# Second rows kept in pairs, their differences formed on GpSimd: attention and router kernel, 1 core

## The reference, cut to what matters

```python
xn = layernorm(x)                                # x: (4, 512, 512), 16 tiles of 128 rows
qkv = silu(xn @ w_qkv.T); gate = sigmoid(xn @ w_gate.T)      # 16 heads of 128
# per head: causal attention with decay in 64-row blocks, a state kv carried over
o = norm_w * o * rsqrt(mean(o * o) + 1e-6)
s = (gate * o) @ w_out.T
w8, i8 = top_k(softmax(xn @ router_weight.T + router_bias), 8)
g = silu(xn * sum(w8) + w8 @ expert_bias[i8])
return x + s * g
```

## Time and profile before

| | |
|---|---|
| three runs | 1120.8, 1121.27, 1123.83 us; median 1121.27 |
| profiled execution | 1121.57 us, its span 1119.7 us |
| mean granted clock of PE | 0.997 |
| PE busy | 1096.1 us, 98% of the span |
| DVE | 844.3 us, 75% |
| ACT | 608.8 us, 54% |
| POOL | 108.2 us, 10% |
| DMA queue of SP | 84.41 MB, 23.4% of 16 engines |
| chain of waits | PE 82%, DVE 13%, ACT 3%, issue 1% |

### The profile page before, as it was taken

The page is one execution under the profiler, slowest core; times in us unless marked ns, Lnnn a source line. Parts: engine busy times, 40 slices in busy tenths (PEclk is TensorE's granted clock), DMA queues, the critical chain, the costliest instruction groups (busy, mean ns, idle before and its releaser), DMA issues.

```text
span 1119.7 us, 16260 instructions
## 1 busy us (share of the span) xinstructions
PE 1096.1 (98%) x6367; PEld 953.0 (85%) x6367; DVE 844.3 (75%) x1637; ACT 608.8 (54%) x1308; POOL 108.2 (10%) x99
## 2 busy tenths in 40 slices
PE   8899999999999999999999999999999999999997
PEld 6788889898898978889788797888988889898886
DVE  7778787776878778786777888868678787766757
ACT  4566474555646455474445655546555564655542
POOL 4001000000000001101010000000000000000002
PEclk8999999999999999999999999999999999999999
DMA  4313121222211223222122341211212032121404
GB/s 136 104 52 104 47 76 60 62 88 57 94 38 58 94 95 112 97 66 85 48 76 79 118 153 57 85 48 48 76 48 76 29 95 66 38 67 47 141 1 132
DMA packets 37566, 85.46 MB, mean 76 GB/s; under 512 B 4320, under 2 KB 8688, under 8 KB 37488
## 3 DMA queue, kind: packets, MB, share of 16 engines
q1 hardware_dynamic: 37488, 84.41, 23.4%
HBM read 73.88 MB, written 14.71 MB: 79 GB/s over the span
## 4 chain that ended last, share of the span: by engine, by line
PE 82%; DVE 13%; ACT 3%; issue 1%; DMA 0%; POOL 0%; SPq 0%; DVEq 0%
PE psR L216 45%; PE psB L216 19%; PE psO L216 8%; PE psS L216 8%; PE psS L647 1%; DVE wvl L394 1%; DVE yacc L790 1%; DVE xl L304 1%; ACT zh L730 1%; DVE gl L394 1%; DVE T L725 1%; DVE T L672 1%; DVE yacc L819 1%; DVE wt L458 1%; ACT ph L674 1%
## 5 line engine op out<-in xcount | busy, mean ns | idle before, releaser
L747 POOL TENSOR_TENSOR ss<-ss,sq 128x512 f32<-128x512 f32 x58 | 78.5, 1353 | 828.6 <-ACT sq L731 828.6
L216 PE MATMUL psR<-xh,gh 128*128 128x512 f32 x384 | 128.6, 416 | 4.8 <-DVE xs L980 2.6
L730 ACT ACTIVATE zh<-T,nw 128x512 fp32r<-128x512 f32 x64 | 46.3, 724 | 136.7 <-DVE T L725 136.7
L216 PE MATMUL psR<-xl,gh 128*128 128x512 f32 x384 | 119.3, 392 | 0.0
L216 PE MATMUL psR<-xh,gl 128*128 128x512 f32 x384 | 118.7, 390 | 0.0
L216 PE MATMUL psB<-xh,gh 128*128 128x512 f32 x288 | 92.8, 403 | 1.2 <-DVE psR L557 1.2
L394 DVE TENSOR_TENSOR gl<-raw,gh 128x256 fp32r<-128x256 f32 x144 | 86.0, 598 | 7.1 <-ACT gh L393 4.7
L216 PE MATMUL psB<-xl,gh 128*128 128x512 f32 x288 | 89.3, 391 | 0.0
L216 PE MATMUL psR<-wvh,xh 128*128 128x256 f32 x512 | 87.3, 293 | 2.0 <-DVE xl L304 1.9
L216 PE MATMUL psB<-xh,gl 128*128 128x512 f32 x288 | 88.8, 390 | 0.0
L674 ACT ACTIVATE ph<-T 128x512 fp32r<-128x512 f32 x64 | 40.5, 632 | 87.6 <-DVE T L672 87.6
(11 more groups left out here) (199 smaller groups left out, 2691.1 us busy)
## 6 DMA issues: line engine op xcount, KB each, us to landing
raw<-w SPq DMA_DIRECT2D x80, 512.0 KB, 3.5
D<-dtab SPq DMA_DIRECT2D x32, 256.0 KB, 2.6
xs<-x SPq DMA_DIRECT2D x28, 256.0 KB, 2.8
dtab<-dscr SPq DMA_DIRECT2D x16, 256.0 KB
gscr<-xs SPq DMA_DIRECT2D x16, 256.0 KB, 2.0
xs<-xnorm SPq DMA_DIRECT2D x16, 256.0 KB, 3.8
out_dram<-yacc SPq DMA_DIRECT2D x16, 256.0 KB, 2.3
xs<-gscr SPq DMA_DIRECT2D x14, 256.0 KB, 3.9
```

Source lines behind the costliest of these rows:

```text
L216: return lambda e: e.matmul(o, l, r, start=start, stop=stop, skip_group_check=shared)
L730: hi = act.do(lambda a: a.activation(zh[:, i, :], T[:, t, :], ACT.Copy, scale=half), z, nw_ev, *zfree)
L747: a = lane.do(lambda g: g.tensor_add(ss[:, j, :], ss[:, j, :], sq[:, :]), q, ss_ev.get(j))
```

## The change

The four differences of each pair of second rows are no longer formed on DVE when the phase changes. They are formed when the rows are kept, on GpSimd, in place in the two row buffers, and stored to a new DRAM tensor `xmixed` (8 tiles of 128 x 512). At the change of phase both `xnorm` and `xmixed` are loaded, one buffer of the ring after the other (`get(count)`).

The eight keepings move from eight consecutive hooks (from (5, 4) on) to four visits: statistics at (0,0), (0,2), (0,3), (1,0), (6,2), (6,3), (6,4), (7,0), for tiles 8, 12, 9, 13, 10, 14, 11, 15. The load stands two hooks ahead of the statistics, or at (0, 0) for the first two. Normalising and the store to `xnorm` now come one hook behind the statistics, and `keep_mixed` comes two hooks behind the second tile of a pair: at (0, 4), (1, 2), (7, 0), (7, 2).

```diff
+    xmixed = nc.dram_tensor("xmixed", (B * N // 2, H), F32, kind="Internal").ap()
...
-            def keep(tt=tt):
-                i, ld = held.pop(tt)
-                stat(tt, i, ld)
-                e = normalise(tt, i, ld)
-                xn_ev[tt] = sp.dma(xs_port[i], xnorm[tt * P:(tt + 1) * P, :], xs[:, i, :], e)
-                xring.give(i, xn_ev[tt])
-
-            later(*step((5, 2), k), load)
-            later(*step((5, 2), k + 2), keep)
...
+        def keep(tt):
+            i, ld = held.pop(tt)
+            e = normalise(tt, i, ld)
+            xn_ev[tt] = sp.dma(xs_port[i], xnorm[tt * P:(tt + 1) * P, :], xs[:, i, :], e)
+            held[("n", tt)] = i
+
+        def keep_mixed(t):
+
+            i, j = held.pop(("n", 8 + t)), held.pop(("n", 12 + t))
+            xa, xb = row(i), row(j)
+            lo, hi = slice(0, 256), slice(256, 512)
+            e = pool.do(lambda g: g.tensor_sub(xa[:, lo], xb[:, lo], xa[:, lo]), xn_ev[8 + t], xn_ev[12 + t])
+            pool.do(lambda g: g.tensor_sub(xb[:, lo], xb[:, lo], xb[:, hi]), e)
+            e2 = pool.do(lambda g: g.tensor_sub(xb[:, hi], xb[:, hi], xa[:, lo]), e)
+            e4 = pool.do(lambda g: g.tensor_sub(xa[:, hi], xa[:, hi], xb[:, hi]), e2)
+            for n, slot, tt in ((2 * t, i, 8 + t), (2 * t + 1, j, 12 + t)):
+                xc_ev[n] = sp.dma(xs_port[slot], xmixed[n * P:(n + 1) * P, :], xs[:, slot, :], e4)
+                xring.give(slot, xc_ev[n])
+
+        KEPT = ((0, 0), (0, 2), (0, 3), (1, 0), (6, 2), (6, 3), (6, 4), (7, 0))
+        for at, tt in zip(KEPT, (8, 12, 9, 13, 10, 14, 11, 15)):
+            later(*step(at, -2 if at[0] or at[1] > 1 else 0), lambda tt=tt: load(tt))
+            later(*at, lambda tt=tt: stat(tt, *held[tt]))
+            later(*step(at), lambda tt=tt: keep(tt))
+        for t in range(4):
+            later(*step(KEPT[2 * t + 1], 2), lambda t=t: keep_mixed(t))
...
         def second_rows():
+
+            def used(i, ev):
+                xring.give(i, ev)
+                get(1)
+
             for t in range(4):
-                (a, lda), (b, ldb) = pairs.pop(t)
-                tile_a(t, a, lda, "B" if t else None)
+                a, na = got.pop((0, t))
+                used(a, place(t, 0, [(s, na) for s in halves(row(a), 0) + halves(row(a), 1)], "B" if t else None))
...
-        later(7, 2, lambda: get(0))
-        later(7, 3, lambda: get(1))
-        later(7, 4, lambda: mingle(0))
+        later(7, 3, lambda: get(4))
+        later(7, 4, lambda: get(2))
```

More of the change, by code:

```diff
@@ L231, in load_x @@
             return i, sp.dma(xs_port[i], xs[:, i, :], x[tt * P:(tt + 1) * P, :], *free)
-        xn_ev, y_ev = {}, {}
+        xn_ev, xc_ev, y_ev = {}, {}, {}
         def row(i):
@@ L1076, in build, with load @@
             router(r, 1, step((1 + 8 * r, 1), 13))
-        for k, tt in enumerate(range(8, 16)):
-            def load(tt=tt):
-                held[tt] = load_x(tt)
-            def keep(tt=tt):
-                i, ld = held.pop(tt)
-                stat(tt, i, ld)
-                e = normalise(tt, i, ld)
-                xn_ev[tt] = sp.dma(xs_port[i], xnorm[tt * P:(tt + 1) * P, :], xs[:, i, :], e)
-                xring.give(i, xn_ev[tt])
-            later(*step((5, 2), k), load)
-            later(*step((5, 2), k + 2), keep)
+        def load(tt):
+            held[tt] = load_x(tt)
+        def keep(tt):
[21 more added lines that the diff above has]
+            later(*step(KEPT[2 * t + 1], 2), lambda t=t: keep_mixed(t))
         for tt in range(8):
@@ L1333, in closing, with get @@
             return steps
[L1335 to L1342, removed]
+        to_get, got = [(n, t) for t in range(4) for n in range(4)], {}
+        def get(count):
+            for _ in range(min(count, len(to_get))):
+                n, t = to_get.pop(0)
+                if n < 2:
+                    got[(n, t)] = load_rows(8 + 4 * n + t)
+                else:
+                    k = 2 * t + n - 2
+                    i, free = xring.take()
+                    got[(n, t)] = i, sp.dma(xs_port[i], xs[:, i, :], xmixed[k * P:(k + 1) * P, :], xc_ev[k], *free)
         def second_rows():
+            def used(i, ev):
+                xring.give(i, ev)
+                get(1)
             for t in range(4):
-                (a, lda), (b, ldb) = pairs.pop(t)
-                tile_a(t, a, lda, "B" if t else None)
+                a, na = got.pop((0, t))
+                used(a, place(t, 0, [(s, na) for s in halves(row(a), 0) + halves(row(a), 1)], "B" if t else None))
                 yield
-                yield from groups_b(t, a, b, ldb, (None, "B" if t < 3 else None, None))
-                if t < 2:
-                    get(t + 2)
+                (b, nb), (c, n1), (d, n2) = (got.pop((n, t)) for n in (1, 2, 3))
+                used(b, place(t, 1, [(s, nb) for s in halves(row(b), 1)] + [(s, n2) for s in halves(row(d), 0)]))
+                yield
+                used(d, place(t, 2, [(s, n1) for s in halves(row(c), 0)] + [(s, n2) for s in halves(row(d), 1)],
+                              "B" if t < 3 else None))
+                yield
+                used(c, place(t, 3, [(s, n1) for s in halves(row(c), 1)]))
+                yield
                 if t < 3:
-                    mingle(t + 1)
                     yield
```

## The result

The changed kernel takes 1129.96 us (median of four runs, 1129.52 to 1130.51) against 1121.5 us (four runs, 1120.80 to 1123.83). The ratio is 1.0072, 95% interval 1.0055 to 1.0089: 8.5 us slower, where 7.1 was forecast. The profiled execution took 1129.56 us, its span is 1127.7.

The account below looks back on a forecast made before the run. PE, busy for 98% of the span, was taken as the bound, so only its waits counted. Losses of 10.1 us and gains of 3.0 made 7.1 slower: 1128.4 us, range 1122.3 to 1132.3 for 8 in 10.

Parts of the forecast that it names:

- Visit 0, 2.3 and 1.1 us: Losses from DVE work ahead of `ql`: 2.3 us at (0, 0), waiting for tile 8's load, and 1.1 at (0, 3).
- The queue, 5.7: At (0, 4), decay blocks behind POOL's subtractions and the `xmixed` stores delay the values' weights of visit 1: 5.7 us lost.
- the straight line between two shapes: POOL's 128x256 subtraction, interpolated between 1.36 us for 128x512 and 0.64 for 128x128: 0.88 each, 3.5 for four.
- POOL's rate: By the skill's page some 0.55 us per 256-element subtraction, making the whole time 1.3 us less; the sum stayed with the rows.
- The port, 1.0: POOL's subtractions hold DVE through the shared port; the second group costs 1.0 us, between 0 and 2.3.
- The clock (rival 3): PE stands still for 5.7 us and its clock falls to 0.50, costing 2 to 3 us: 1131; chance 0.13.
- Visits 5 and 6, 0.9: Gain of 0.9 us from work leaving hook (6, 0), nothing counted at the other old hooks; bounds 0 and 0.95.
- The change of phase, 2.1: Gain of 2.1 us from 16 subtractions leaving DVE there: PE's waits for `yacc` and part of those for low parts.
- The bound of 2.5: Upper bound on the change-of-phase gain: PE's waits there for `yacc`, 1.5 us, and low parts, 1.0, both whole.

Follow-up runs that it names:

- experiment 2: The changed kernel with tile 8's statistics moved to (0, 1) and its normalising to (0, 2), its load staying at (0, 0): 1127.58 us, ratio 1.0056.
- experiment 1: The changed kernel with the decay-table blocks of visit 2 registered at (0, 4) ahead of the `xnorm` and `xmixed` stores: 1123.62 us, ratio 1.0016.
- experiment 5: As experiment 1, but with the four subtractions of each pair done on DVE at the same hooks: 1123.26 us, ratio 1.0012.
- experiment 6: As experiment 1, but without the subtractions of the first two pairs, in visits 0 and 1; all stores stay: 1122.7 us, ratio 1.0009.
- experiment 3: The changed kernel with 20 additional 128x512 matmuls ahead of the first product of the values in visit 1: 1128.52 us, ratio 1.0064.
- experiment 4: The kernel before with its rows kept at the eight new hooks, differences still on DVE, nothing stored to `xmixed`: 1126.56 us, ratio 1.0045.

## Why the prediction was right

The time lay in the range, on the side and by the mechanism forecast. Its steps, against the table:

- **Visit 0, 2.3 and 1.1 us: right.** 3.5 measured. PE waited 2.45 and 0.81, and experiment 2 gave the first back alone (2.4). The load landed 6.5 us after its issue, close to the 6.0 of the earlier trace rows.
- **The queue, 5.7: right in mechanism and nearly in size.** The blocks start at 97.92, where 94.8 and the 3.4 lost before make 98.2. POOL's four subtractions took 3.3 us from start to end, forecast 3.5; the straight line between two shapes was good. The weights were on hand 16.7 us after the blocks, forecast 15.9. Counted from the first `ss` addition, the first product of the values started 6.1 us late (24.85 us for 18.79). Of that PE stood 4.6 for the weights, and the rest it came late itself. Experiment 1 moved only the blocks and got 6.3 back. By the Trainium skill ("DMA: Bandwidth & Descriptors", Queues, rings and completion order) the completion of the weights is counted on each DMA engine only behind that engine's earlier writes. The runs agree: in the kernel before, in the change and in experiment 1 the weights were on hand 15.9, 16.7 and 17.8 us after the blocks had started.
- **POOL's rate.** The Trainium skill ("GPSIMD Engine Reference", Elementwise) gives about 2.6 cycles an element for two inputs, by which the prediction estimated 0.55 us for 256 elements. Here that was too low: 0.73 to 0.92 in the first two groups.
- **The port, 1.0: mis-sized, with a term missing.** Queue and port together were put at 6.7 for visit 1, and it lost 8.9: the 6.1 up to the first product of the values, and 2.8 behind it, where the port was to cost 1.0. The hold itself is real, 1.1 and 1.5 us of DVE in the two groups (experiment 5), and the first group was hidden by the late weights, as forecast. But the subtractions are the smaller part of the 2.8: behind that product experiment 1 loses 1.8 and experiment 6, without subtractions, still 1.35. I had set the keeping hooks of visit 1 at nothing. The last 1.0 is there only where the weights are late, and what makes it stays open.
- **The clock (rival 3) came about, and was not what decided.** It fell to 0.50, as that rival said, and made one product 2.3 us longer; experiment 3 took the fall away and the visit won 0.2. I had added the two as if they lay end to end.
- **Visits 5 and 6, 0.9: too small.** 2.1 was won. I had counted the longest wait, 0.95, and nothing at the other old hooks. The old hooks shared a form, though: statistics, a stand of 0.67 for `rstd` and normalising, 2.2 us of DVE together, and the gain comes in three steps of 0.7, 1.2 and 0.6 us, with 0.4 lost between. Which hook gave which step was not tried. The keepings from (6, 2) on stand at hooks that were in use before, and cost no more there than the old ones: from 471 to 551 us of the old trace the delay begins and ends at 10.3.
- **The change of phase, 2.1: close.** 2.7 was won. The bound of 2.5, all waits of the earlier trace rows, was too tight: the low parts kept 0.9 of their waits, and 2.7 came back though only 1.6 of waits are gone. The other 1.1 is in PE's busy time: between the same two `ss` additions (530.19 and 637.67 in the kernel before) it was busy 103.2 us, and 102.1 after. A busy PE isn't one at its peak, and a table of waits is no upper bound on what an engine's relief is worth. Which matmuls it was is not assigned to a row.

In sum: forecast 10.1 lost and 3.0 won, measured 12.4 and 4.8. The losses were a fifth too small and the gains over a third, and the errors partly cancelled.

## What to carry to other kernels

When work moves, price the queue that it passes before the engine that it leaves: two DMAs, held by one wait behind a GpSimd chain, cost more than all the rest. Put slow transfers ahead of whatever can block the issuing engine. And work put on a second engine isn't hidden because that engine is idle: here a group on GpSimd held DVE for 1.1 to 1.5 us, where DVE would have needed 1.6 to do it itself. Whether two small pieces at one hook cost more than the same pieces two hooks apart stays open: one pair of tiles cost 1.1 us more so, the other nothing.

## What the hardware did that I had not expected

- Stands of PE of 4.6 and 4.3 us brought the granted clock down to 0.50. Of the shorter ones in visit 0, 2.4 us left it at 1.00 in the changed kernel, and 2.5 and 2.3 us in experiments 5 and 4 brought it to 0.50. There it cost 1.4 us; in visit 1, by experiment 3, 0.2 of 2.3.
- The time that SP takes to issue a DMA is uneven: in the changed kernel SP took 6.06 us to issue the load of `D` behind the blocks, in experiment 1 the store of `xnorm` there took 4.16 and `D` 0.40. In these two traces the long issue is that of the first DMA behind the blocks, whichever it is; those behind it took 0.3 to 0.8.
- A DVE instruction with one SBUF tensor input can be held by POOL too. Normalising took 1.50 us at 119.25 while POOL added from 119.11 to 120.47, and 0.55 in the earlier trace rows. Normalising took 0.96 us while POOL ran its first subtractions. The two rows of the changed kernel, DVE and then POOL:

```profile
119.25 1.50 DVE L278 TENSOR_SCALAR xs<-xs,mv,rstd 128x512 f32<-128x512 f32 x1
...
119.11 1.36 POOL L748 TENSOR_TENSOR ss<-ss,sq 128x512 f32<-128x512 f32 x1 [13.73 <-ACT sq L732]
```
